# The end of the third source turn: the fourth head's attention ahead of its two experts, and the fourth chunk's norm, scores and gate ahead of the third chunk's norm and source rows

## The reference, cut to what matters

```
x = x + gnn0(layernorm(x), adj)   # 4 heads of 32: softmax over leaky_relu(src_i + dst_j) where adj
x = x + ffn0(layernorm(x))        # 8 experts 128->512->128, top 2 by a gate, biases b1, b2
x = x + gnn1(layernorm(x), adj)   # one attention from the mean of 4 heads' leaky_relu(s1_i + s2_j)
x = x + ffn1(layernorm(x))        # 128->256, two layers of 256->256 routed by block of 32 rows, ->128
```

## Time and profile before

| | |
|---|---|
| time, median of 3 runs | 642.82 us (642.39 to 643.41) |
| the profiled execution, its time | 641.88 us |
| the profiled execution, its span | 640.1 us |
| TensorE matmuls busy | 545.5 us (85%) |
| TensorE weight loads busy | 427.7 us (67%) |
| VectorE busy | 515.6 us (81%) |
| ScalarE busy | 372.2 us (58%) |
| GpSimd busy | 175.9 us (27%) |
| mean granted TensorE clock | 0.942 |

### The profile page before, as it was taken

The page is one execution under the profiler, slowest core; times in us unless marked ns, Lnnn a source line. Parts: engine busy times, 40 slices in busy tenths (PEclk is TensorE's granted clock), DMA queues, the critical chain, the costliest instruction groups (busy, mean ns, idle before and its releaser), DMA issues.

```text
span 640.1 us, 13281 instructions
## 1 busy us (share of the span) xinstructions
PE 545.5 (85%) x5082; PEld 427.7 (67%) x5082; DVE 515.6 (81%) x907; ACT 372.2 (58%) x756; POOL 175.9 (27%) x186
## 2 busy tenths in 40 slices
PE   1876984999999999799998897999996756999985
PEld 1675972878775877766685575588786555566753
DVE  6799969997787857699949738899999898999420
ACT  1796893768885777685756836633421301565473
POOL 3301000075211100993522010121314000365741
PEclk9987995989998899998998999899999878899999
DMA  6484860022165156999599224020102844475750
GB/s 142 85 161 76 215 153 2 17 83 68 33 199 198 38 195 215 186 211 237 119 209 110 67 69 131 2 67 1 66 1 80 303 134 139 120 208 175 202 165 16
DMA packets 48857, 78.36 MB, mean 122 GB/s; under 512 B 5406, under 2 KB 24870, under 8 KB 48794
## 3 DMA queue, kind: packets, MB, share of 16 engines
q1 hardware_dynamic: 30714, 52.02, 26.0%
q0 software_dynamic: 15488, 22.02, 20.1%
q10 hardware_dynamic: 2592, 3.48, 2.0%
HBM read 80.61 MB, written 22.06 MB: 160 GB/s over the span
## 4 chain that ended last, share of the span: by engine, by line
PE 52%; DVE 26%; ACT 14%; issue 5%; DMA 1%; ACTq 1%; POOL 0%; SPq 0%; DVEq 0%
DVE arena L1633 15%; PE bank L698 11%; PE bank L710 11%; PE bank L627 10%; PE bank L863 5%; ACT arena L1137 5%; PE bank L824 2%; ACT maskT L1006 2%; PE bank L658 2%; PE bank L900 2%; ACT ysb L1089 1%; PE bank L808 1%; PE bank L576 1%; PE bank L603 1%; DVE arena L1489 1%
## 5 line engine op out<-in xcount | busy, mean ns | idle before, releaser
L483 POOL TENSOR_TENSOR x<-x,ysb 128x512 f32<-128x512 f32 x36 | 74.7, 2076 | 249.8 <-ACT ysb L1089 237.7
L1137 ACT ACTIVATE arena<-heads,nd 128x512 bf16<-128x512 f32 x176 | 112.0, 723 | 22.9 <-PE bank L627 22.3
L698 PE MATMUL bank<-hTc,arena 128*128 128x512 f32 x192 | 92.9, 638 | 5.6 <-ACT reg_c L1078 5.6
L1633 DVE SCALAR_TENSOR_TENSOR arena<-reg_b,nd,arena 128x1536 f32<-128x1536 f32 x48 | 92.0, 1979 | 0.0
L710 PEld LDWEIGHTS bank<-arena,reg_c 128*128 128x128 f32 x768 | 87.6, 192 | 4.8 <-issue 4.7
L710 PE MATMUL bank<-arena,reg_c 128*128 128x128 f32 x768 | 88.5, 275 | 0.0
L627 PEld LDWEIGHTS bank<-reg_b,arena 128*128 128x128 bf16 x1536 | 73.7, 99 | 7.1 <-DVE arena L1489 4.0
L1078 ACT ACTIVATE reg_c<-bank,b 128x512 f32<-128x512 f32 x96 | 65.0, 686 | 22.8 <-PE bank L698 22.6
L627 PE MATMUL bank<-reg_b,arena 128*128 128x99 bf16 x1536 | 74.9, 211 | 3.7 <-DVE arena L1489 3.7
L1089 ACT ACTIVATE ysb<-bank,comb 128x128 f32<-128x128 f32 x128 | 36.5, 367 | 65.0 <-PE bank L909 39.9
L1475 DVE TENSOR_TENSOR arena<-maskT,arena 128x2048 bf16<-128x2048 bf16 x36 | 50.4, 1401 | 27.4 <-ACT arena L1137 27.4
(11 more groups left out here) (195 smaller groups left out, 846.6 us busy)
## 6 DMA issues: line engine op xcount, KB each, us to landing
maskT<-routed_sums SPq DMA_DIRECT2D x48, 256.0 KB, 3.2
reg_c<-in_adj POOLq DMA_DIRECT2D x16, 512.0 KB, 7.9
arena<-in_w1T SPq DMA_DIRECT2D x16, 512.0 KB, 4.0
arena<-in_w2T SPq DMA_DIRECT2D x16, 512.0 KB, 4.9
routed_sums<-in_wsT SPq DMA_DIRECT2D x32, 256.0 KB, 5.6
routed_sums<-in_wrT POOLq DMA_DIRECT2D x32, 256.0 KB, 13.9
arena<-routed_sums SPq DMA_DIRECT2D x32, 256.0 KB, 3.0
routed_sums<-ident POOLq DMA_DIRECT2D x4, 1024.0 KB, 12.6
```

The costliest lines, as they stand in the source:

```text
L483: nc.gpsimd.tensor_tensor(xi, xi, ysb[:, e % 3, :].rearrange("p (t d) -> p t d", d=P), ALU.add).then_inc(s_acc, 1)
L698: mm(bank[b][:, :], w1[:, s, e % 2, c * P:(c + 1) * P], hTc[:, :], start=True, stop=True).then_inc(full[b], 1)
L1137: last = af(ind[:, q, b, j, :], sbc[:, h, :], ACT.Relu, bias=nd[:, q * QT + j, h:h + 1], scale=BIG)
L1633: last = v.scalar_tensor_tensor(p, row, nd[:, t, h:h + 1], p if h else maskT[:, t, columns], ALU.max, ALU.mult)
```

## The change

On all engines the tail of the third turn is put in another order. TensorE makes both row scores one after the other (chunk 1's into bank 2 and not bank 6), then `attend(3)`, then `second_layer(3)`. After the projections of chunks 0 and 1 it makes the transposes and gate scores of chunk 3 and `first(0)`, and only then the transposes, source rows and projection of chunk 2. ScalarE follows that order; its `exponents(1)` and `scale_values(0)` stand between the gate scores and `first(0)`. VectorE merges head 3 and normalises chunk 3 into `xn` before it waits for the last expert of chunk 2 and normalises that into `odiv`. `best` moves ahead of the first product, and `gate` from after the third head of the first pair to after its first. On SyncE the load of expert pair 1 moves behind the six transfers of row scores. No arithmetic is added or removed.

```diff
@@ SyncE
-                    load_pair(c, h, c < C - 1 or h < 2)
                     if c == C - 1 and h == 1:
                         for r in range(2):
...
+                    load_pair(c, h, c < C - 1 or h < 2)
@@ TensorE
-                pe.wait_ge(ev["hTc"], (2 * C - 1, 2 * C, 2 * C + 1, 2 * C + 3)[c] + 1 if s else c + 1)
+                pe.wait_ge(ev["hTc"], (2 * C - 1, 2 * C, 2 * C + 2, 2 * C + 3)[c] + 1 if s else c + 1)
...
                         row_scores(0, 7)
+                        row_scores(1, 2)
+                        attend(h)
                     second_layer(h)
-                    if h == H - 1:
-                        row_scores(1, 6)
-                attend(h)
+                if h < H - 1:
+                    attend(h)
...
             project(1, 1, (5, 7))
-            ln_transpose(6, xn)
+            scores(xn)
+            first(0)
+            ln_transpose(6, odiv)
+            pe.wait_ge(ev["hTc"], 2 * C + 3)
+            source_rows1(2)
             project(1, 2, (5, 7))
-            source_rows1(2)
-            scores(odiv)
-            first(0)
             first(1)
@@ ScalarE
                         row_scores(0, 7)
+                        row_scores(1, 2)
+                        head(C - 1, h)
                     for e in (2 * h, 2 * h + 1):
                         second_layer(e)
-                    if h == H - 1:
-                        row_scores(1, 6)
-                head(C - 1, h)
+                if h < H - 1:
+                    head(C - 1, h)
...
             project1(1)
-            ln_out(2)
-            project1(2)
-            source_rows1(2)
+            act.wait_ge(s_spill, 16 * (C + 1))
+            scores()
             exponents(1)
             scale_values(0)
-            act.wait_ge(s_spill, 16 * (C + 1))
-            scores()
             first(0)
+            ln_out(2)
+            source_rows1(2)
+            project1(2)
             first(1)
             gate()
@@ VectorE
             replicate(1)
+            merge(C - 1, H - 1)
+            norm(C - 1, 2 * C)
             dve.wait_ge(s_acc, (C - 1) * (E0 + 1))
-            norm(2, 2 * C)
-            merge(C - 1, H - 1)
-            norm(C - 1, 2 * C + 1, odiv)
+            norm(2, 2 * C + 1, odiv)
...
+            best(C - 1, 2 * C - 1)
             dve.wait_ge(ev["rows"], 2 * H)
-            wide_pair(0, range(2))
-            best(C - 1, 2 * C - 1)
-            wide_pair(0, range(2, 3))
+            wide_pair(0, range(1))
             gate(C - 1, 2 * C - 1)
-            wide_pair(0, range(3, H))
+            wide_pair(0, range(1, H))
```

## The result

| | before | after |
|---|---|---|
| median of 18 runs | 642.49 us (637.16 to 645.45) | 646.69 us (640.66 to 650.17) |
| ratio of after to before | | 1.008, 95% interval 1.0051 to 1.0109 |
| profiled execution, time and span | 641.88, 640.1 | 644.58, 642.8 |

The forecast was 647.3 us, which is 4.5 over the median of 642.82 that it was worked out from and 4.8 over 642.49. A second comparison of the same two kernels gave 1.0045 (1.0008 to 1.0083). By these ratios the change costs 5.1 us in the first comparison and 2.9 in the second, and by the medians 4.2 and 1.1 (643.67 against 642.58), so times alone don't give the size well. The trace tells it more sharply.

What follows compares the result with a forecast made beforehand. VectorE's gapless run of second-layer products was taken as the bound. First product 7.3 us later, `best` 2.8 back, gate 0.3 more: 4.8, taken as 4.5, upon the 642.82 median gives 647.3 us; range 644.0 to 651.0.

Steps and rivals of the forecast that it cites:

- The main step: Late source rows of chunk 2 move VectorE's first product from 395.19 to 402.5; kernel 4.5 us slower; chance 0.64.
- What comes back: VectorE's first pair: `best` outside it returns 2.8 us, gate adds 0.3, so 7.3 becomes 4.8 us, taken as 4.5.
- Bank 5: TensorE's projection of chunk 0 waits for expert 7's weighed copy in that bank, starting at 387.2, 1.4 us later.
- The norms: VectorE: chunk 3 normalised at 387.2, transposes at 389.6; chunk 2's norm waits 1.3 us and ends at 393.6.
- The score product: Chunk 3's score products on TensorE start at 391.0, their copy 1.50 us later; no wait for `best`.
- The source rows: Chunk 2's rows stand behind `first(0)` and 2.1 us of ScalarE exponents and scaled values; first product 7.3 us later.
- The gate: VectorE's wait before the gate for ScalarE's exponential: 1.9 us, where it was 1.62.
- The transfers: Row loads there by 390 at the latest, a gain of some 5 us nobody collects: products wait for source rows.
- TensorE after that: Expert 0's second layer begins 2.1 us earlier on TensorE, which VectorE, 4.5 us late, cannot use.
- The slow clock: Rival: TensorE's waits bring half speed into the source rows, up to 3.5 us on top, 650.8 us; chance 0.12.
- relief by GpSimd: Rival, no change: GpSimd additions fall into the norm or a wait instead of products, 4 us back, 643.3; chance 0.12.
- The slots: Rival, faster: slots freed by `attend_wide` pace VectorE's pairs, third pair absorbs the late start, 640.7 us; chance 0.12.

Runs made afterwards that it cites:

- Experiment 4: Changed kernel with `exponents(1)` and `scale_values(0)` on ScalarE moved from ahead of `first(0)` to behind the gate's exponential: 645.14 us, 1.0047 to the kernel before.
- experiment 3: Changed kernel with chunk 2's transposes, source rows and projection ahead of `first(0)`, and the gate's exponential directly behind the source rows: 644.19 us, 1.0044 to before.
- experiment 5: Changed kernel with the load of expert pair 1 on SyncE back ahead of the row transfers: 647.46 us, 1.0077 to the kernel before.
- experiment 6: Kernel before with only the first half: both row scores and head 3's attention ahead of the experts, pair's load behind the transfers: 648.59 us, 1.0114.
- experiment 7: Changed kernel with only the second half: experts ahead of head 3's attention as before, chunk 3 still first, chunk 2 second: 656.17 us, 1.0202 to before.
- experiment 8: Kernel before with the gate's exponential on ScalarE ahead of `first(1)`: 641.97 us, 0.9968.
- experiment 9: Kernel before with the gate's exponential ahead of `first(1)` and chunk 2's source rows ahead of its projection on TensorE and ScalarE: 642.16 us, 0.9993.
- experiment 10: Kernel of experiment 8 with `attend_wide(0)` ahead of `first(3)` on TensorE: 642.62 us, 0.9982 to the kernel before.
- experiment 11: Kernel before with chunk 3's transposed copy and gate scores ahead of `exponents(1)` and `scale_values(0)` on ScalarE: 640.99 us, 0.9978.
- experiment 12: Kernel before with source rows ahead of the projection, scores ahead of `exponents(1)` and `scale_values(0)`, these behind `first(1)`, gate's exponential behind `first(0)`: 639.67 us, 0.9955.

## Why the prediction was right, and where its steps were not

The predicted first product at 402.5, measured against the merge at 371.45, is a distance of 31.0 us. It was 30.62. The sum of 4.5 us stands against 4.73 in the distance and 4.2 between the medians. The main step, late source rows of chunk 2 with everything behind them on VectorE, is what the runs show. That the sum came so near is in part luck: 0.7 us of the 4.73 were not in it (see "What comes back"), and without them the distance would have grown by 4.0. Step by step:

* *Bank 5.* Forecast 1.4 us of new wait, 1.39 shown. No run takes this wait away. Without it the transposes of chunk 3 could have come at most 0.5 us sooner, upon the norm that they use.
* *The norms.* Chunk 3's norm ended at 387.6, 0.5 us ahead of TensorE's transposes at 388.08, where the prediction had 2.4 us of cover. During GpSimd's two additions one small operation of it took 1.13 us and not 0.17, and its last step 2.07 and not 1.11. For chunk 3 this was just hidden. For chunk 2 it took the place of the 1.3 us wait that was forecast: VectorE came to that norm 0.5 us after the last addition had ended. The norm of chunk 2 ended at 22.5 us after the merge against 22.2 forecast.
* *The score product.* I took 1.50 us from its start to its copy and it was 1.10, since its clock did not fall. This is the few tenths that the prediction had set aside.
* *The source rows.* The place was right and half of the mechanism was wrong. I had named ScalarE's 2.1 us ahead of `first(0)`. Experiment 4 gives them 0.56, since TensorE's four products (390.51 to 394.59) take nearly as long by themselves. The two walks give nearly the same time. Of the 6.88 us by which "first" grew, 1.99 are the wait of the transposes behind `first(0)`. The other 4.89 come with the later norm of chunk 2. The 1.99 us could not be had by moving `first(0)` away, since experiment 3 got 0.19.
* *The gate.* Wait of 1.9 us forecast, 1.49 shown.
* *What comes back.* First grew by 6.88 and norm by 4.73, 2.15 less. `best`, no longer between the products, accounts for 2.77. The gate's wait gave 0.13 more, and 0.7 went the other way into the products themselves, which were busy for 66.1 + 24.3 = 90.4 us ahead of the norm. In the kernel before the same view has 67.5 + 22.2 = 89.7. With 6.88 - 2.77 - 0.13 + 0.7 = 4.7 the distance is accounted for. The groups by line, 385 to 493.5 us (busy us, mean ns of one):

```profile
L1636 DVE SCALAR_TENSOR_TENSOR arena<-reg_b,nd,arena 128x1536 f32<-128x1536 f32 x34 | 66.1, 2006 | 0.0
...
L1636 DVE SCALAR_TENSOR_TENSOR arena<-reg_b,nd,maskT 128x1536 f32<-128x1536 f32 x12 | 24.3, 2060 | 5.4 <-ACT reg_b L1028 5.4
```

  The 0.7 are the last two products ahead of the norm. In both kernels nine products took 2.82 us, so the additions cost the same. In the changed kernel the last two took 2.16 us each, beside two casts of GpSimd (line 523). In the kernel before these began only after the norm. The products (ns min/median/max), and the casts after and before:

```profile
L1636 DVE SCALAR_TENSOR_TENSOR arena<-reg_b,nd,arena x2: 2156/2156/2157, 488.6 to 490.7; 128x1536 f32<-128x1536 f32 x2
```

```profile
487.90 3.36 POOL L523 CAST routing<-onehot 128x512 bf16<-128x512 f32 x2 [0.66 <-DMA arena<-in_bo]
...
492.28 1.16 POOL L523 CAST routing<-onehot 128x512 bf16<-128x512 f32 x2 [2.15 <-DMA arena<-in_bo]
```

* *The transfers.* "A gain that nobody collects" was wrong by 0.8 us (experiment 5).
* *TensorE after that.* The second layer of expert 0 began 34.6 us after the merge in place of 37.6, so 3.0 us sooner where 2.1 were forecast. As forecast, VectorE could not use it.
* *The rivals.* The slow clock did not come in the reordered part of the changed kernel, where TensorE waited 1.39 us at the most. It came behind waits of 2.24, 3.91 and 6.15 us in experiments 3, 6 and 7. No relief by GpSimd showed, as nine products met additions in both orders. The slots did not absorb the late start, as VectorE's unbroken products had said. The small slack that spoke for this case was real and decided experiments 8 to 10. The prediction put it at 431.10 against 431.04, but the third pair began later than that, 0.40 us behind the end of `attend_wide(0)`, and experiment 8 found 0.28 of it to gain:

```profile
431.44 3.54 DVE L1633 SCALAR_TENSOR_TENSOR arena<-reg_b,nd,maskT 128x1536 f32<-128x1536 f32 x2
```

The two halves cost 7.4 and 13.4 us alone and 4.7 together. Each half is repaired in part by the other: attention first makes chunk 3's norm early, and with it there is something for TensorE to do while chunk 2's norm waits for its last expert. What neither repairs is that the source rows of chunk 2 gate VectorE's longest run, and that the change puts their last expert behind the attention and their products behind `first(0)`. That is why it is slower than before.

What stays open: the size in time. The two comparisons give 2.9 and 5.1 us (1.0045 and 1.008), with single runs 10 us apart, and I did not find out what in the first 370 us makes the merge move by 8 us from run to run. The place of that spread is shown, its cause is not. The mean granted clock from 0 to 368 us was 0.95 in the profiles with the two earliest merges (368.15 and 368.32) and 0.93 in the one with the latest (376.46), so the clock can be a part of it.

## What to carry to other kernels

When a reordering ahead of a long run on one engine is judged, find the operand that the run's first instruction needs, and count everything that the change puts in front of it on every engine. Filling an engine's idle time earlier was worth nothing here, because that operand got later. Measure distances from a common instruction ahead of the edit; here they repeated to 0.01 us where times spread by 10. And once the run's start has been moved forward, look for the second bound right away, since here it was 0.3 us behind the first. Before work is taken out of the queue ahead of a needed operand, ask whether it was what kept TensorE's clock up (experiment 3).

## What the runs showed of the hardware that was not expected

An idle stretch of TensorE cost nearly as much again afterwards, or more. After 2.24 us of waiting, in a stretch of 4 us with 1.02 busy, four source row products took 5.45 us and not 3.86, so 1.59 longer (experiment 3). Shortening one wait from 2.60 to 0.75 us took 2.4 us off the eight products behind it (experiment 11). The clock had fallen behind that wait in all five profiles that have a wait of 2.6 to 2.7 us there (before and experiments 6 and 8 to 10), and it stayed at 1.00 in both with the wait of 0.75 us (experiments 11 and 12).

A product of VectorE that meets a GpSimd addition took 2.82 us in every kernel, as in the earlier trace rows, and 2.16 us beside GpSimd's casts. Two such casts in turn took 3.36 us together beside products, and 1.16 behind the norm.
